# The last quarter of an attention block in two parts, the first moved ahead between two head groups

## What is computed

```python
h = _layernorm(x, axis=-1) * (1 + ca) + sa
x = x + ga * _L0_attn_ref(h, L0_attn_qkv_w, L0_attn_qkv_b, L0_attn_out_w, L0_attn_out_b)
h = _layernorm(x, axis=-1) * (1 + cb) + sb
x = x + gb * _L0_ffn_ref(h, L0_ffn_w_router, L0_ffn_w_fc, L0_ffn_w_proj)
...
# in the attention: causal softmax over 1024 keys, heads of 8 columns
scores = jnp.einsum('bhqd,bhkd->bhqk', q, k) * scale
scores = jnp.where(causal_mask, -jnp.inf, scores)
attn = jax.nn.softmax(scores, axis=-1)
out = jnp.einsum('bhqk,bhkd->bhqd', attn, v)
```

## Time and profile before

| what | value |
|---|---|
| median of 3 runs | 363.34 us (363.15 to 363.46) |
| the profiled execution | 361.05 us |
| its span | 359.3 us |
| TensorE busy in it | 334.0 us (93%) |
| VectorE / ScalarE / GpSimd busy | 258.5 / 207.7 / 111.0 us |

### The profile page before, as it was taken

How to read it: one execution, slowest core, us unless ns; L and a number is a source line. 1 busy time by engine, 2 the same in 40 slices (tenths; PEclk the granted TensorE clock), 3 DMA queues, 4 the chain that set the end, 5 groups by cost and what they waited for, 6 DMA issues and landing times.

```text
span 359.3 us, 6875 instructions
## 1 busy us (share of the span) xinstructions
PE 334.0 (93%) x2360; PEld 160.3 (45%) x2360; DVE 258.5 (72%) x563; ACT 207.7 (58%) x399; POOL 111.0 (31%) x191
## 2 busy tenths in 40 slices
PE   6999889999899999999999999999999999899886
PEld 3545345444443433533634434445434445445454
DVE  4956977986999787678688797677987778332353
ACT  5250166753456575876466666854767666685251
POOL 3937363524411234301302013002114033344121
PEclk9999999999999999999999999999999999999999
DMA  6547353302400002330230402300000000000000
GB/s 210 184 116 183 85 127 101 82 16 71 115 1 0 3 3 73 94 88 0 70 97 20 117 2 60 79 0 32 0 2 4 2 3 2 3 0 3 29 2 29
DMA packets 12641, 18.96 MB, mean 53 GB/s; under 512 B 3496, under 2 KB 8488, under 8 KB 12608
## 3 DMA queue, kind: packets, MB, share of 16 engines
q1 hardware_dynamic: 12320, 18.14, 18.3%
q10 hardware_dynamic: 288, 0.39, 0.3%
HBM read 12.98 MB, written 5.24 MB: 51 GB/s over the span
## 4 chain that ended last, share of the span: by engine, by line
PE 64%; DVE 10%; issue 10%; POOL 2%; ACT 2%; SPq 1%; DMA 1%; ACTq 0%; DVEq 0%; POOLq 0%
PE ps_o L1080 17%; PE ps L1060 13%; PE ps L1043 13%; PE ps L1014 4%; DVE tmax L878 4%; PE ps L1001 4%; PE ps L1038 3%; PE ps L950 2%; PE ps L1022 1%; PE ps L1007 1%; DVE rot L774 1%; PE ps L941 1%; SPq L419 1%; ACT pt L674 1%; PE ps L968 1%
## 5 line engine op out<-in xcount | busy, mean ns | idle before, releaser
L878 DVE TENSOR_REDUCE tmax<-ps 128x1 f32<-128x512 f32 (+3 forms) x304 | 185.7, 656 | 57.0 <-PE ps L1043 56.8
L674 ACT ACTIVATE pt<-ps 128x512 f32<-128x512 f32 (+1 forms) x304 | 161.1, 576 | 97.0 <-PE ps L1060 95.4
L1060 PE MATMUL ps<-qst,kst 128*128 128x512 bf16 (+3 forms) x384 | 110.3, 326 | 4.7 <-DVE rot L774 2.2
L1043 PE MATMUL ps<-kst,qst 128*128 128x128 bf16 (+3 forms) x576 | 113.2, 274 | 0.7 <-DVE fg L854 0.3
L1080 PE MATMUL ps_o<-pt,v_sb 128*32 128x512 f32 (+3 forms) x768 | 78.7, 496 | 2.0 <-ACT pt L674 1.1
L1043 PEld LDWEIGHTS ps<-kst,qst 128*128 128x128 bf16 x576 | 49.0, 98 | 65.5 <-DVE tmax L878 16.1
L570 POOL TENSOR_SCALAR_AFFINE_SELECT pt<-pt 128x512 f32<-128x512 f32 x64 | 40.3, 639 | 64.5 <-ACT pt L674 64.2
L1060 PEld LDWEIGHTS ps<-qst,kst 128*128 128x128 bf16 x384 | 34.8, 98 | 30.2 <-issue 5.3
L1022 PE MATMUL ps<-maska,identb 128*128 128x512 bf16 x124 | 35.4, 393 | 3.3 <-POOL maska L489 3.3
L533 POOL CAST negp<-negm 128x16 bf16<-128x16 f32 x16 | 3.1, 196 | 93.1 <-DVE negm L795 92.9
L1080 PEld LDWEIGHTS ps_o<-pt,v_sb 128*32 128x32 f32 x768 | 16.9, 108 | 29.2 <-ACT pt L674 16.1
(11 more groups left out here) (103 smaller groups left out, 256.2 us busy)
## 6 DMA issues: line engine op xcount, KB each, us to landing
qst<-qparts SPq DMA_DIRECT2D x48, 96.0 KB
kst<-kparts SPq DMA_DIRECT2D x48, 96.0 KB
qparts<-part SPq DMA_DIRECT2D x16, 96.0 KB, 1.9
kparts<-part SPq DMA_DIRECT2D x16, 96.0 KB, 1.9
xs<-in_x SPq DMA_DIRECT2D x4, 256.0 KB, 7.0
rope_sb<-in_rope SPq DMA_DIRECT2D x2, 512.0 KB, 6.0
qparts<-part SPq DMA_DIRECT2D x16, 64.0 KB, 1.8
out<-y SPq DMA_DIRECT2D x3, 256.0 KB, 2.0
```

What stands on the lines that cost most here:

```text
L674: act.activation(pt[:, G % NP, h0:h0 + nh, 0:w], src, ACT.Exp, scale=SCALE).then_inc(s_exp, 1)
L878: dve.tensor_reduce(dst, src, AX.X, ALU.max).then_inc(s_max, 1)
L1043: last = pe.matmul(dst[:, j * nk:(j + 1) * nk], qst[:, half, h, r * P:r * P + P], kst[:, kh, h, k0:k0 + nk], start=(kind != "diag"), stop= ...
L1060: last = pe.matmul(dst[:, j * w:(j + 1) * w], kst[:, kh, h, kt * P:kt * P + P], qst[:, half, h, c0:HALF], start=True, stop=True)
```

## The change

The last unit becomes two units of 256 rows with their own steps: (1,0,0) with rows 0 to 255, and (1,0,1) with rows 256 to 511. `TURNS` sets the new order: units (0,0) and (0,1) as before, then (1,1) with head groups 0 and 1, then (1,0,0) with four steps, then (1,1) with head groups 2 and 3, then (1,0,1) with four steps: 20 steps. A step of the first part has 3 banks in pass A and 3 in pass B, one of the second part 8 and 7 (before: 11 and 11 in a step of the whole unit). The post steps of the first part follow its own steps. Each short step has its own max1 and max2, and its maxima are written by two DMAs instead of one. The loads of (1,0) now come first, at two slots behind the last times-v of unit (0,1)'s group, and those of (1,1) twelve slots later. The squares that go to GpSimd are those of the last two entries of `POSTS`, (1,1) and the second part.

```diff
-STEPS = [(b, half, g) for b, half in UNITS for g in range(NG)]
+POSTS = [(0, 0, 0), (0, 1, 0), (1, 0, 0), (1, 1, 0), (1, 0, 1)]
+TURNS = [((0, 0, 0), range(NG)), ((0, 1, 0), range(NG)), ((1, 1, 0), (0, 1)), ((1, 0, 0), range(NG)), ((1, 1, 0), (2, 3)),
+         ((1, 0, 1), range(NG))]
+STEPS = [u[0:2] + (g,) + PIECES[u[0:2]][u[2]] for u, gs in TURNS for g in gs]
...
-    for r in range(TU):
+    for r in range(t0, t1):
         jobs.append(("diag", r, 0, HG, P))
...
-    for kt in range(TU):
-        n = HALF - kt * P
-        nh = max(1, HALF // n) if n < 384 else 1
-        out.append((kt, half, kt * P, [(h, nh) for h in range(0, HG, nh)]))
+        out += [(kt, 0, (P * t0, P * t1), [(h, 1) for h in range(HG)]) for kt in range(TU)]
+    for kt in range(t1):
+        c0, c1 = P * max(kt, t0), P * t1
+        nh = HALF // (c1 - c0)
+        out.append((kt, half, (c0, c1), [(h, nh) for h in range(0, HG, nh)]))
...
+def is_joined(s, gi):
+
+    b, half, _, t0, t1 = STEPS[s]
+    kt, kh = groups_b(half, t0, t1)[gi][0:2]
+    return kt % 2 == 0 if (b, half) == PARTED else kt == TU - 2 and kh == half
...
-        at = max(a_end[6 + g] + MAX_LAG, done[(1, 1)] + 1)
-        assert v_end[4 + g] < at < a_end[7 + g] - LEAD
-        put(at, "load", (1, 1), g)
-        put(at + 12, "load", (1, 0), g)
-    for s, (b, half, g) in enumerate(STEPS):
-        at = v_end[s] + O_LAG
+        at = put(max(v_end[4 + g] + 2, done[(1, 0)] + 1), "load", (1, 0), g)
+        at = put(max(at + 12, done[(1, 1)] + 1), "load", (1, 1), g)
...
-            for name in POST if (b, half) != UNITS[-1] else POST_LAST:
+            for name in POST if s + 1 < len(STEPS) else POST_LAST:
...
-                for piece in range(len(PIECES[(b, half)])):
-                    at = put(at, name, (b, half, piece))
+                at = put(at, name, (b, half, k))
...
-        squares, squares_pool = [], [(n + (k,), c) for n in UNITS[-2:] for c in (1, 3)
-                                     for k in range(len(PIECES[n]))]
+        squares, squares_pool = [], [(st[1], int(st[0][1])) for st in order
+                                     if st[0] in ("a1", "a3") and st[1] in POSTS[-2:]]
...
+                else:
+                    for r in range(t1 - t0):
+                        sp.dma_start(qst[ROWS:ROWSM, half, heads, P * (t0 + r):P * (t0 + r) + P],
+                                     negt[n * r:n * r + n, s % 2, :]).then_inc(s_mstack[s % 2], 16)
...
-                        if st[0] == "n3" or st[1] == last_piece(len(UNITS) - 1):
+                        if st[0] == "n3" or st[1] == POSTS[-1]:
                             keep_warm(WARM_POST[st[0]])
```

More of the change, by code:

```diff
@@ L121, in plan @@
     a_at, a_end, n = {}, [], 0
-    for s, (b, half, g) in enumerate(STEPS):
-        for job in bank_jobs_a(half):
+    for s, (b, half, g, t0, t1) in enumerate(STEPS):
+        for job in bank_jobs_a(half, t0, t1):
             a_at[n] = (s, job)
@@ L128, in plan @@
     slot, v_end, joined = 0, [], []
-    for s, (b, half, g) in enumerate(STEPS):
+    for s, (b, half, g, t0, t1) in enumerate(STEPS):
         slot = max(slot, a_end[s] + LEAD)
-        for gi, grp in enumerate(groups_b(half)):
+        for gi, grp in enumerate(groups_b(half, t0, t1)):
             for bank in grp[3]:
@@ L135, in plan @@
             joined.append((s, gi, grp))
-            if grp[0] != TU - 2 or grp[1] != half:
+            if not is_joined(s, gi):
                 v_at[slot - 1 + PVLAG], joined = joined, []
@@ L143, in put @@
         busy = ON_POOL.get(stage[0], 0)
-        if need and stage[0] in HIDDEN + ("y0", "y1") and stage[1][0:2] == UNITS[-1]:
+        if need and stage[0] in HIDDEN + ("y0", "y1") and stage[1] == UNITS[-1] + (1,):
             hold = 1
@@ L205, in adaln_block @@
     bank_no = {i: n for n, i in enumerate(sorted(b_at))}
+    tri_no = {}
+    for grp in sorted(group_no, key=group_no.get):
+        if is_diagonal(*grp):
+            tri_no[grp] = len(tri_no)
+    post_no = {u: n for n, u in enumerate(POSTS)}
+    xb_no = {st[1]: n for n, st in enumerate(st for st in order if st[0] == "xb")}
+    n_order = [st for st in order if st[0] in ("n1", "n3")]
     prep_no = {u: n for n, u in enumerate(PREPS)}
-    unit_no = {u: n for n, u in enumerate(UNITS)}
     pe_at = {i - 1: sts for i, sts in stages.items()}
@@ L365, in tiles, with on_of, rows_of_maxima, whole @@
             return PIECES[u[0:2]][u[2]]
-        def last_piece(n):
-            return UNITS[n] + (len(PIECES[UNITS[n]]) - 1,)
+        def on_of(u):
+            return on_first if u == POSTS[2] else on
+        def rows_of_maxima(s):
+            return HG * (STEPS[s][4] - STEPS[s][3])
+        def whole(s):
+            return STEPS[s][3:] == (0, TU)
+        def rows_sent(s):
+            return 16 * sum(1 if whole(r) else STEPS[r][4] - STEPS[r][3] for r in range(s % 2, s + 1, 2))
+        def last_group(s):
+            return group_no[(s, len(groups_b(STEPS[s][1], *STEPS[s][3:])) - 1)]
         def split(eng, name, u):
@@ L561, in zero_future @@
             def zero_future(s, gi, grp):
-                kt, khalf, c0, banks = grp
-                if khalf != STEPS[s][1] or (STEPS[s][1] and gi < TU):
+                if not is_diagonal(s, gi):
                     return
@@ L632, in run @@
                     s = u
[L633 to L636, removed]
+                    act.wait_ge(s_pv, last_group(s) + 1)
+                    before = [r for r in range(s) if STEPS[r][2] == STEPS[s][2]]
+                    if before:
+                        wait_read(act, f"n{STEPS[s][2]}", SPAN_OF[before[-1]])
+                    cols = slice(P * STEPS[s][3], P * STEPS[s][4])
+                    act.activation(ot[:, STEPS[s][2] // 2, cols], ps_o[:, 0, cols], ACT.Copy).then_inc(s_ot, 1)
                 if name in POST:
@@ L1025, in stack_ready @@
             def stack_ready(s):
-                b, half, g = STEPS[s]
+                b, half, g = STEPS[s][0:3]
                 for hf in ((0, 1) if half or b else (0,)):
@@ L1079, in times_v @@
                     c = (HG * g + j) * VS + (VW, 0)[g % 2]
-                    last = pe.matmul(ps_o[32 * j:32 * j + 32, 0, c0:HALF], v_sb[:, TU * (2 * b + kh) + kt, c:c + 32],
-                                     pt[:, G % NP, j, 0:HALF - c0], start=(gi == 0 and g % 2 == 0),
+                    last = pe.matmul(ps_o[32 * j:32 * j + 32, 0, c0:c1], v_sb[:, TU * (2 * b + kh) + kt, c:c + 32],
+                                     pt[:, G % NP, j, 0:c1 - c0], start=(gi == 0 and g % 2 == 0),
                                      stop=(gi == n - 1 and g % 2 == 1))
```

134 lines of the change are left out of this document (78 added, 56 removed).

## The result

The changed kernel takes 370.83 us in the median (369.48 to 371.85) against 363.25 for the kernel before: a ratio of 1.0215, 95% interval [1.0174, 1.0256]. The forecast was +2.3 us, the result is +7.6, and 370.83 lies above the range's 368.4. Its sign was right, its size was not.

The account below looks back on a forecast made before the run. TensorE, 93% busy at full clock, was taken as the bound, then one chain at the end. Terms: +3.2 us up to the last times-v, -0.9 behind it, +2.3 in all; 363.3 became 365.6, range 362.2 to 368.4.

Parts of the forecast that it names:

- the first part's post steps: Moved from the end into slots 258 to 295, among the passes: 7.4 us added, between 6.9 and 8.4.
- the short steps: Four more max1 and max2 on TensorE, before the last times-v: +1.0 us, between 0.7 and 2.0.
- the leftovers: (1,1)'s `m1`, `m2`, `m3`, `y0`, `y1` leave the stretch before the last times-v for the end: -4.7 us there.
- the 14.0: TensorE time of the last unit's post steps when they stand alone at the end, in us.
- The rival of the holes: Faster: the first part's matmuls fall into times-v waits in slots 258 to 295; -1.8 us, 361.5; chance 0.17.
- the cover of GpSimd's wait: `a3` and `m0` between the last two times-v calls cover the last one's wait for GpSimd: -0.5 us at best.
- The rival of dear short steps: Slower yet: four chains from maxima to max2 in 12 slots wait 0.5 each, banks too: +2, 367.6; chance 0.10.
- To `rt`: From the last times-v to the start of `rt`: 12.55 us instead of 8.8, 3.7 later than before.
- To the end: From `rt` to the end of the span, with one piece left: 10.4 us instead of 15.0.
- the 10.4 us behind `rt`: After `rt`: 5.4 of TensorE work, 2.5 of waits, 2.5 from the last add to the end.
- the stated -3.0 to +0.5: Ends for the whole end behind the last times-v, forecast -0.9 us: `y1` and `y0` find gaps, or the chain waits more.
- a lower granted clock: Sign of being wrong; as rival, matmuls behind `rt` slow at 1.2 GHz: +2.7 us, 368.3; chance 0.05.

Follow-up runs that it names:

- that run: Kernel before with the last unit's split steps in line, not moved, and nine matmuls without use ahead of (1,1)'s `h2`: 363.42 us, ratio 1.0015.
- the one with the leftovers: Kernel before with (1,1)'s post steps from `m1` held back until pass B's last bank is through: 361.24 us, ratio 0.998.
- the first filled kernel: Changed kernel with matmuls without use added behind (1,1)'s `y1` and among the single piece's steps: 368.55 us, ratio 1.0144 to the kernel before.

## Why the prediction was wrong, and where it was right

**Ahead of the last times-v, +5.5 for +3.2.** Three prices, each measured apart, close the sum: 8.1 for the first part's post steps, 0.7 for the short steps, -3.4 for the leftovers: +5.4. The last two were measured in the order of the kernel before, not in their new place, so that the sum closes better than its parts can claim.

- The first part's post steps were put at 7.4 between 6.9 and 8.4; 8.1 is within. The work is 6.7, half of the 14.0 without n3, which the run left in place. (The terms given for 14.0 add up to 14.2; with the 0.38 us that the matmul without use takes in the trace they give 14.0.) The waits are what was low: 0.4 was taken for them, since the chain's operations are shorter, and 1.4 came, the whole of the upper end. The rival of the holes, which would have it below 4.4, falls; unit (0,1)'s price was the right evidence. The rule of the Trainium skill, "Perfetto Trace Analysis", section "Identifying the Most-Contended Engine", by which busy weight loads and not busy matmuls tell how near the engine is to its peak, promised room here; the 8.1 us speak against it in this stretch.
- The short steps (+1.0) and the cover of GpSimd's wait (-0.5) were +0.5 together; with the clock held they are +0.7. The rival of dear short steps (+2 more) falls. In that run and in the one with the leftovers alike the last times-v no longer waits for GpSimd, so in which of the two prices the -0.5 is contained stays open.
- "`m1`, `m2`, `m3`, `y0` and `y1` fall into the end: ... I take 4.7" is a term with the wrong currency. The work leaves, as forecast, but the price of TensorE's time was read in slots 236 to 263, where both passes run and TensorE is 100% busy, and used in the stretch where pass B runs alone and TensorE is at 91% (29.45 of 32.20). There some 4.5 us of work gave back 3.4: this step failed. The waits that took the rest stood in rows of the trace, times-v calls behind ScalarE's exponentials and behind GpSimd; with the work gone they grew from 1.00 to 2.19 us.

**To `rt`, +3.5 for +3.7.** Right in size and in mechanism: `ln` behind `y1`, `y1` behind the filling.

**To the end, -0.9 for -4.6.** This is the larger miss. The step that failed is the 10.4 us behind `rt`: it counts the matmuls there at the full clock, so that the clock stands in the sum at nothing. With the clock held the stretch is 11.1, 0.7 more for the waits of the single chain and the added matmuls; the whole end is then 23.4 us, -0.4 against before, within the stated -3.0 to +0.5. The other 2.9 is the clock, at 0.50 from about 355 us on, and a lower granted clock was among the signs of being wrong that the forecast named. As a rival it was named, placed ("the matmuls behind `rt`") and priced near (+2.7 for 2.9), in part by luck, since the halving in that price has no working; its chance was 0.05. That rested on "no row here shows it fall", but the kernel before keeps its clock with 13 matmuls that were put there, behind `out`, and the walk itself found that in the new end they stand ahead of `y1` and no longer next to the wait before `h2`. The evidence needed was the cover that had moved, not a fall in a trace that had the cover.

With the leftovers at -3.4 and the chain at 8.1 the forecast would have been some 367.6, and with the clock some 370.5. The larger errors all pointed the same way, and the range was too narrow above by 2.4 us; the forecast's own ends reached +6.3, 369.6, where the range stopped at 368.4.

## What to carry to other kernels

Price moved work in the stretch that it leaves as well as in the one that it enters: where an engine has waits of its own, work taken out returns only part of its time (here some three quarters), and work put in where the engine is full costs all of it and the waits of its chain. Before shortening a tail, look for what keeps TensorE's clock up there: when the work behind a wait is halved or filling loses its place, reckon the rest of the tail at half clock as the likely case, not as a rival; three kernels here lost it in their tails, in all runs or in most. And a slow kernel with a fallen clock says nothing on any other theory until the run is repeated with the clock held. Before time without work is called a wait, the count of matmuls is compared with that of another trace of the same program: missing records made 5.05 us out of 3.92 here.

## What the runs showed of the hardware

No single wait decides on the clock. In the changed kernel's profile TensorE waited 1.71 us before (1,1)'s `h2` and kept 1.00; in the first filled kernel, the same program up to there, the same wait of 1.71 was followed by 0.58 and 0.50; 2.38 and 3.37 us were followed by 0.50. In the changed kernel's end the longest wait ahead of the fall was 1.34 us, with 0.66 behind it (the 0.52 came as the clock was down), and the clock fell in all four runs (mean 0.981 to 0.983). What decides stays open. The Trainium skill, "TensorE: Matmul & The Clock Gate", section "A second HAM failure mode: psum-queue depth-cycling", tells of a kernel in which short but frequent idles between groups of matmuls made the clock go down and up again. The fall in this end agrees, with waits of 1.34 and 0.66 us; a rise is not seen in it.

Once fallen, the clock stayed at 0.50 for about ten us of dense matmuls in one kernel (311 to 321 us, TensorE busy for 9.47), for at least five in another (347 to 352 us, busy throughout), and to the end where the matmuls stood apart (356 to 368 us, busy for 8.88). A fallen clock cost less than the matmuls' time over again: behind `rt` it cost 2.9 us, where the forecast counts 5.4 us of TensorE work at the full clock. A step of another engine kept its time: the last add on DVE takes 0.42 at the half clock as in the earlier trace rows.
